# Attention and feed-forward block on one core: projections and transposes moved from full-height to 64-row TensorE tiles, attention outputs turned by VectorE

## The reference

```
h   = LN(x);  q, k, v = h @ w_q.T, h @ w_k.T, h @ w_v.T
a   = softmax(q k^T / 4) v   (per batch and head) ;  y = a @ w_o.T
x   = x + LN(y)
h   = LN(x);  prev = h shifted by one token (zeros for the first)
xr  = mu_r*h + (1-mu_r)*prev ;  xk = mu_k*h + (1-mu_k)*prev
r   = sigmoid(xr @ W_r.T) ;  kk = relu(xk @ W_k.T)^2
out = x + LN(r * (kk @ W_v.T))
```

## Time and profile before

| | |
|---|---|
| median of 3 runs | 1445.39 us |
| the profiled execution | 1448.0 us, its span 1446.2 us |
| PE, matmuls | 1354.5 us busy (94%), 8916 records |
| PE, weight loads | 607.8 us (42%) |
| ACT | 1015.3 us (70%) |
| DVE | 858.2 us (59%) |
| POOL | 299.2 us (21%) |
| granted TensorE clock, mean over the span | 0.983 |

### The profile page before, as it was taken

The page is one execution under the profiler, slowest core; times in us unless marked ns, Lnnn a source line. Parts: engine busy times, 40 slices in busy tenths (PEclk is TensorE's granted clock), DMA queues, the critical chain, the costliest instruction groups (busy, mean ns, idle before and its releaser), DMA issues.

```text
span 1446.2 us, 21872 instructions
## 1 busy us (share of the span) xinstructions
PE 1354.5 (94%) x8916; PEld 607.8 (42%) x8916; DVE 858.2 (59%) x1738; ACT 1015.3 (70%) x1080; POOL 299.2 (21%) x366
## 2 busy tenths in 40 slices
PE   3889999999999999999999999999999999999974
PEld 2433454444443444344443444444444444433433
DVE  5442575567647585565755666466754647463747
ACT  2558767777677677777777776776777777788751
POOL 7100211213111221212112222111311121211221
PEclk9999999999999999999999999999999999999996
DMA  3562534215232345115441152422442054301010
GB/s 131 143 161 86 113 64 103 59 60 116 63 86 59 108 82 106 43 44 132 88 103 49 56 130 45 103 59 75 101 94 61 23 131 88 75 2 30 1 30 15
DMA packets 61311, 112.79 MB, mean 78 GB/s; under 512 B 6400, under 2 KB 31232, under 8 KB 61184
## 3 DMA queue, kind: packets, MB, share of 16 engines
q1 hardware_dynamic: 61184, 111.05, 31.9%
HBM read 69.08 MB, written 41.94 MB: 77 GB/s over the span
## 4 chain that ended last, share of the span: by engine, by line
PE 79%; ACT 12%; DVE 7%; issue 1%; POOL 0%; DMA 0%
PE O L410 28%; PE M L193 25%; PE S L391 21%; ACT PT L398 11%; PE M L465 2%; PE M L442 2%; DVE A L561 1%; PE M L235 1%; DVE scratch L560 1%; DVE C L188 1%; DVE xA L227 1%; DVE scratch L576 0%; DVE B L188 0%; DVE p L264 0%; DVE Z L188 0%
## 5 line engine op out<-in xcount | busy, mean ns | idle before, releaser
L398 ACT ACTIVATE PT<-S 128x1024 f32<-128x1024 f32 x1024 | 983.9, 1024 | 318.1 <-PE S L391 318.1
L410 PE MATMUL O<-PT,V 128*17 128x512 f32 x4096 | 541.0, 600 | 0.0
L391 PE MATMUL S<-QS,KS 50*128 50x512 f32 x2048 | 417.3, 465 | 34.7 <-ACT PT L398 30.2
L391 PEld LDWEIGHTS S<-QS,KS 50*128 50x128 f32 x2048 | 169.8, 184 | 295.6 <-ACT PT L398 211.6
L193 PE MATMUL M<-WH,B 128*128 128x256 f32 x768 | 165.9, 298 | 14.0 <-DVE B L565 6.4
L193 PEld LDWEIGHTS M<-WH,B 128*128 128x128 f32 x768 | 127.6, 193 | 97.0 <-issue 39.5
L505 POOL TENSOR_SCALAR veh<-mvh 128x2 f32<-128x2 f32 x96 | 21.2, 221 | 583.3 <-DVE mvh L503 582.9
L410 PEld LDWEIGHTS O<-PT,V 128*17 128x17 f32 x4096 | 68.0, 95 | 160.1 <-issue 159.9
L193 PE MATMUL M<-WL,B 128*128 128x256 f32 x384 | 109.4, 285 | 0.0
L193 PE MATMUL M<-xnT,WH 128*128 128x512 f32 x256 | 92.8, 445 | 9.8 <-DVE xnT L243 9.8
L637 DVE RECIPROCAL Z<-Z 128x512 f32<-128x512 f32 x30 | 100.6, 3353 | 1.0
(11 more groups left out here) (101 smaller groups left out, 1263.6 us busy)
## 6 DMA issues: line engine op xcount, KB each, us to landing
scr<-p SPq DMA_DIRECT2D x124, 256.0 KB
QS<-scr SPq DMA_DIRECT2D x60, 256.0 KB, 5.0
KS<-scr SPq DMA_DIRECT2D x60, 256.0 KB, 7.0
QS<-scr SPq DMA_DIRECT2D x68, 128.0 KB, 4.3
KS<-scr SPq DMA_DIRECT2D x68, 128.0 KB, 7.3
xA<-x_dram SPq DMA_DIRECT2D x16, 512.0 KB, 7.1
xB<-x_dram SPq DMA_DIRECT2D x16, 512.0 KB, 7.6
out_dram<-xB SPq DMA_DIRECT2D x15, 512.0 KB, 3.5
```

Of the source, the lines that this page charges most:

```text
L391: fn = lambda e, p=p, a=a, rows=rows: e.matmul(PS[p][:, a, :], KS[qd][rows, p, kt * 128:kt * 128 + 128], QS[qd][rows, p, hf * 512:hf * 512 ...
L398: e_fn = lambda e, p=p: e.activation(PT[i % 2][:, 2 * p:2 * p + 2, :], PS[p][:, :, :], ACT.Exp, scale=SCALE)
L410: fn = lambda e, j=j: e.matmul(PO[g % 2][32 * j:32 * j + 17, :], V[b % 2][:, kt, 4 * qd + j, :], PT[i % 2][:, j, :], start=(kt == 0), stop ...
```

## The change

All projections and transposes are cut in two halves of 64 rows (a = 0 and a = 1), as the scores are. Half 0 of a block runs in rows 0 to 63 and half 1 in rows 64 to 127, both adding into the same bank; half 1 starts only after half 0 has finished, so that meanwhile half 0 of the next block runs beside it. There are three PM banks instead of two, and one PO bank instead of two. `pump`, called once a step between `scores(i+1)` and `values(i)`, gives each tile matmuls worth a quota of 0.68 (1.3 in the first 8 steps). A block enters when the operations that make its input have been issued. Orders by hand now list blocks alone; what follows a block is spread over the next steps at each REST.

The outputs of a quad are turned by DVE's transposes of 32x32 blocks out of PO (T), divided, and after each second quad turned once more and split into cT (the split's difference is POOL's); the order of w_o's rows is permuted to fit. The mixes are made in the order k, r with the first on A and C; the reciprocal of 512 columns is cut in two. The k activations go to C instead of Bf. o_x, o_xr, o_xk, o_act, o_sig and o_out go into what follows y, z, k, r and v. Spreads are issued at steps 12, 18, 26 instead of 16, 24, 27 (the first batch's at 9 instead of 12).

```diff
-STEPS, RATE = 29.00, 0.750
+TERMS = ((0, 0), (0, 1), (1, 0))
...
-        PO = [ctx.enter_context(nc.psum_tensor(f"O{i}", [128, 512], F32)) for i in range(2)]
-        PM = [ctx.enter_context(nc.psum_tensor(f"M{i}", [128, 512], F32)) for i in range(2)]
+        PO = ctx.enter_context(nc.psum_tensor("O", [128, 512], F32))
+        PM = [ctx.enter_context(nc.psum_tensor(f"M{i}", [128, 512], F32)) for i in range(3)]
...
+        def put(a):
+
+            cost, fn, waits = tile[a].pop(0)
+            spent[a] += cost
+            if tile[a]:
+                pe.quiet(fn, *waits)
+            else:
+                now[a].token = pe.op(fn, *waits)
+            if a == 0:
+                for block in halfway:
+                    block.behind += cost
+            if not tile[a]:
+                block, now[a] = now[a], None
+                if a == 0:
+                    halfway.append(block)
+                else:
+                    until_rest(block.done(block.bank, PM[block.bank], block.token))
+
+        def begin(a, wait):
+
+            if a == 0:
+                if not waiting or len(halfway) > 1 or (halfway and now[1] is not None):
+                    return False
+                ready, free = waiting[0].ready(), bank_free[made[0] % 3]
+                if ready is None or free is None:
+                    return False
+                block = waiting.popleft()
+                block.bank = made[0] % 3
+                bank_free[block.bank] = None
+                made[0] += 1
+                tile[0] = [(cost, fn, ()) for cost, fn in block.half(PM[block.bank], 0)]
+                tile[0][0] = (*tile[0][0][:2], (*ready, *free))
+            else:
+
+
+                if not halfway or not (halfway[0].behind > .3 or wait):
+                    return False
+                block = halfway.popleft()
+                tile[1] = [(cost, fn, ()) for cost, fn in block.half(PM[block.bank], 1)]
+                tile[1][0] = (*tile[1][0][:2], (block.token,))
+            now[a] = block
+            return True
+
+        def pump(quota):
+
+            due[0] += quota
+            for a in range(2):
+                spent[a] = max(spent[a], due[0] - 2 * quota)
+            while True:
+                stuck = 0
+                for a in sorted(range(2), key=lambda a: spent[a]):
+                    if not tile[a] and not begin(a, not tile[0]):
+                        stuck += 1
+                    elif spent[a] + tile[a][0][0] / 2 > due[0]:
+                        stuck += 1
+                    else:
+                        put(a)
+                        break
+                if stuck == 2:
+                    return
+
...
+        def feature_half(name, mt, moving):
+
+            n = W_NAMES.index(name)
+
+            def half(m, a):
+                rows, out = rows_of(a), []
+                for k, (c, (i, j)) in enumerate(itertools.product(range(2), TERMS)):
+                    w = (WH, WL)[i][rows, n, c, mt * 128:mt * 128 + 128]
+                    out.append((.216, lambda e, k=k, w=w, v=moving(j, c, rows): e.matmul(
+                        m[:, :], w, v, start=(a == 0 and k == 0), stop=(a == 1 and k == 5))))
+                return out
+            return half
+
+        def token_half(name, still):
+
+            n = W_NAMES.index(name)
+
+            def half(m, a):
+                rows, out = rows_of(a), []
+                for k, (t, c, (i, j)) in enumerate(itertools.product(range(2), range(2), TERMS)):
+                    w = (WH, WL)[j][rows, n, c, :]
+                    out.append((.117, lambda e, k=k, t=t, w=w, v=still(i, c, t, rows): e.matmul(
+                        m[:, t * 256:t * 256 + 256], v, w, start=(a == 0 and k == 0),
+                        stop=(a == 1 and k % 6 == 5), skip_group_check=True)))
+                return out
+            return half
+
+        def turn_half(src):
+
+            def half(m, a):
+                rows = rows_of(a)
+                return [(.109, lambda e, t=t: e.transpose(m[:, t * 128 + 64 * a:t * 128 + 64 * a + 64],
+                                                          src(t, rows), ident[rows, rows])) for t in range(4)]
+            return half
 
...
-                d = dve.op(lambda e: e.tensor_copy(On[g % 2][:, :], PO[g % 2][:, :]), pv_of[i], on_read.get(g - 2),
-                           split_of["wr"])
-                acc_free[g % 2] = d
-                on_ready[g] = d
-
+                until_rest(quad(g, qd))
+
+
+
+        def quad(g, qd):
+            at, half = T[g % 2], qd % 2
+            view = at[:, :].rearrange("p (y r) -> p y r", r=32)
+            d = dve.op(lambda e: e.transpose(at[:, :], PO[:, :]), pv_of[8 * g + 7], tk.get(("T", g % 2)),
+                       split_of["wr"])
+            tk["acc_free"] = d
+            if qd < 3:
+                yield REST
+            d = dve.op(lambda e: e.reciprocal(rec[:, :], view[:, :, 16]), d, tk.get("rec_read"))
+            over = rec[:, :].unsqueeze(2).to_broadcast([128, 16, 16])
+            d = dve.op(lambda e: e.tensor_tensor(CC[:, qd // 2, :, 16 * half:16 * half + 16], view[:, :, 0:16], over,
+                                                 ALU.mult), d, tk.get("CC_read"), *part_read[2])
+            tk["rec_read"] = tk["T", g % 2] = d
+            if not half:
+                return
+            yield REST
+            cols = slice(512 * (qd // 2), 512 * (qd // 2) + 512)
+            d = dve.op(lambda e: e.transpose(at[:, :], CC[:, qd // 2, :, :].rearrange("p y r -> p (y r)")), d)
+            tk["CC_read"] = d
+            d = copy(cT[0][:, cols], at[:, :], d, tk.get("cT_read"))
+            d = side().op(lambda e: e.tensor_tensor(cT[1][:, cols], at[:, :], cT[0][:, cols].bitcast(F32),
+                                                    ALU.subtract), d)
+            tk["T", g % 2] = tk["cT", g // 4, qd // 2] = d
 
...
+                d = copy(C[0][:, cols], A[:, cols], k, tk.get("C_read"))
+                tk["xk", u, c] = side().op(lambda e: e.tensor_tensor(
+                    C[1][:, cols], A[:, cols], C[0][:, cols].bitcast(F32), ALU.subtract), d)
+                lent_to.append((k1, diff, k))
...
+        FIRST = "V2 V3 Q10 K10 Q11 K11"
+        EVEN = "T00 T10 y0 y1 T01 T11 Q00 K00 z0 z1 Q01 K01 k0 k1 r0 r1 V0 v0 v1"
+        ODD = "Q10 K10 y0 y1 Q11 K11 z0 z1 V1 V2 k0 k1 r0 r1 V3 v0 v1"
+        QUOTA, FIRST_QUOTA = .68, 1.3
-        SPREAD_AT = (16, 24, 27)
+        SPREAD_AT = (12, 18, 26)
...
             for s in range(32):
                 i = 32 * u + s
                 if i + 1 < len(steps):
                     scores(i + 1)
-                values(i)
                 if s == 0 and u > 0:
                     load_xb(u - 1)
-                if s in NEW:
-                    o_turn(u, NEW.index(s))()
-                    spent += COST["ot"]
-                if cost == REST:
-                    cost = next(pieces, None)
-                while cost is not None and (cost <= 0 or spent + cost / 2 <= rate * (s + 1) or s == 31):
-                    if cost == REST and s < 31:
-                        break
-                    spent += max(cost, 0.0)
-                    cost = next(pieces, None)
+                pump(FIRST_QUOTA if u == 0 and s < 8 else QUOTA)
+                values(i)
+                again, resting[:] = resting[:], []
+                for work in again:
+                    until_rest(work)
                 if u == 0 and 3 <= s < 7:
                     split_weights([W_NAMES[s]])
-                if (u, s) == (0, 12):
+                if (u, s) == (0, 9):
                     spread(0, 2)
                     spread(0, 3)
...
```

More of the change, by code:

```diff
@@ new lines, in sandwich_kernel, with __init__, until_rest @@
+        tile = [[], []]
+        now = [None, None]
+        spent, due = [0.0, 0.0], [0.0]
+        made = [0]
+        resting = []
+        class Block:
+            def __init__(self, half, ready, done):
+                self.half, self.ready, self.done = half, ready, done
+                self.behind = 0.0
+        def until_rest(work):
+            for said in work or ():
+                if said == REST:
+                    resting.append(work)
+                    return
[15 more added lines that the diff above has]
+                    until_rest(block.done(block.bank, PM[block.bank], block.token))
@@ L499, in norm_stats, with have, ready @@
+        def have(*keys, more=(), queued=()):
+            def ready():
+                found = [tk.get(key) for key in keys]
+                return None if None in found or not all(key in tk for key in queued) else (*found, *(split_of[name] for name in more))
+            return ready
         def norm_stats(g, src, *ready):
@@ L551, in run, with mix, for_k @@
                 tk["z", c] = [d, d0]
-            return run
-        def o_xr(u, c):
-            def run():
+                if c:
+                    yield from mix(u)
```

(44 more changed lines are left out.)

395 lines of the change are left out of this document (142 added, 253 removed).

## The result

The changed kernel takes 1740.96 us (median of 4 runs, 1731.23 to 1748.49), the kernel before beside it 1444.89 (4 runs): a ratio of 1.2045, 95% interval 1.1974 to 1.2116. The prediction said 1343, 1282 to 1414. Lines Lnnn are now lines of the changed kernel: S L494, exps L501, O L513, matmuls of feature blocks L268 (512 columns a half) and of token blocks L281 (256), transposes on PE L291, DVE's transposes L530 and L544.

A forecast was written before the change was run, and what follows sets the result against it. The prediction took PE, busy 94% of the span, as the bound. Steps 845+321+36+22+8+5 = 1237, head 52, tail 55 and 1.8 around gave 1346, as median of runs 1343 us, range 1282 to 1414.

The forecast's parts named there:

- (2): Projection matmuls on PE split into 64-row halves: a pair priced as one whole matmul, 321 us with transposes; at worst 321 more.
- (4): Even dealing of matmuls to the tiles by quota 0.68 per step: unevenness costs 36 us, upper bound 72.
- rival D: Halves on PE do not overlap when weights change each time: 1664 us if none do, chance 0.03.
- (7): Half 1 waits for its half 0, PE's queue behind it: 8 us together with operand waits, bounds 0 and 30.
- rival A: Waits for DVE, at the single O bank and at projections' banks and operands, take the gain: 1415 us, chance 0.13.
- (5): DVE's load stays near 850 us, transposes 0.69 each; the difference moved to POOL, 1.69 each, is hidden.
- (3): Scores and projections on PE share a tile form, so entering projections costs nothing: step 2.28 us, 1166 for 512 steps.
- Rival B: Nothing is saved on PE's mode changes, each step pays 0.20 for entering projections: 1445 us, no change, chance 0.04.
- Rival C: PE is bound by its number of instructions, 59 ns each: step 2.51 us, total 1461, chance 0.06.
- (6): One PSUM bank for O instead of two, PE waiting for DVE to turn it: 22 us, bounds 0 and 96.
- (8): Head and tail, where blocks must run a half alone at each end: +6.5 and +2, making 52 and 55 us.
- (1): Turns of O and of the concatenated heads leave PE: 384 transposes, 42 us less.

The follow-up runs named there:

- couple_late2: Changed kernel with two blocks at a time, their halves laid in pairs, blocks taken up two steps late, quota 0.70: 1436.57 us, 0.9923 of the kernel before.
- couple_bulk: couple_late2 with one line changed, so that of every couple first tile 0's halves are queued, then tile 1's: 1656.92 us.
- paired: Changed kernel with another dealing: a stuck empty tile saves up no time, and tile 0 may start a block while one is halfway: 1546.11 us.
- first: Changed kernel, but an empty tile 0 is given its next block before tile 1 is asked: 1641.07 us.
- whole: Changed kernel with projection and transpose blocks at full height (128 rows, no halves), the rest of the change kept: 1486.82 us.
- whole_late2: whole with blocks taken up two steps after their operands were queued and quota 0.72 instead of 0.68: 1451.44 us.
- the three couples shown above: couple_late2 and two variants of it: couples begun a step after their banks' copies, with other edits (1484.25 us); y groups behind the second transposes (1462.01 us).

## Why the prediction was wrong, point by point

**(2), the price of halves: this step failed**, together with **(4)**. It rested on what pairs of scores show and took for granted that the halves of M would lie beside each other as those do. The hardware part holds: pairs start together, and 3964 halves cost what 1981 whole ones did (`couple_late2`), with new weights each time. What I did not do is follow `pump` into the queue. (4) priced unevenness as 36 us, with 72 as its bound and "a lone half block" in it; the queue makes 498-321 = 177. I had written the whole loss, 321 us, into (2) as its worst end, but left it out of the range and gave it, as rival D, 0.03, by a mechanism (weights change) that isn't the one. The order is: `couple_bulk` costs 220 by nothing but order, and `paired` takes back 195, of which some 43 belong to (7).

**(7), the end of half 0: 8 us expected, bounds 0 and 30.** "The plan puts 0.3 of other matmuls between" is true only where `wait` is false, which holds for 24 of 288. In the steps 194 have 0.3 to 0.6 us more between their second scores and O than the queue's prices; they sum to 94 us. Removing most of it gave 100 (`first`).

**Operands, rival A's mechanism, were there too.** 29 steps have over 1 us more than their prices, 89 us, the low clock behind a stand included. Six of them, 4.8 to 4.9 each, stand at the beginning of a batch, where y waits for POOL's difference of cT (32.5 us in all, the longest wait 4.7). Part (5) called that difference "hidden by the blocks queued between the last quad and y". POOL takes 1.30 each, less than the 1.69 assumed, but the cover was missing where y came next. What late take-up brought, 35 us in `whole` and 46 in `paired`, is about what such steps lose: their excess falls from 83 to 49 in the one and from 114 to 65 in the other. The chain after at one such place:

```profile
465.25 1.27 POOL cT L547
...
466.57 0.37 PE M L281
```

No matmul starts between 462.93 and 466.57. The clock is the third value from the end (ahead of DMA share and GB/s) in these stretches before, around and behind it:

```profile
455.00:462.90 7.90, 7.53 (x64) 4.08 (x57) 4.40 (x15) 6.06 (x7) 3.15 (x5) 1.00 0.00 1
464.50:471.30 6.80, 4.73 (x21) 2.62 (x22) 3.35 (x5) 0.91 (x1) 1.66 (x2) 0.50 0.83 187
471.40:480.00 8.60, 8.48 (x68) 4.89 (x67) 1.97 (x6) 5.60 (x7) 2.22 (x3) 1.00 0.79 154
```

It falls to 0.50 (1.2 GHz) in the stand and stays there for 4.7 us of work behind it.

**Account of the steps after,** from the starts, with M by the model: S and O 845, M 498, the two kinds of wait with smaller ones 202, slower S 25 and O 20: 1590, against 1588.9. Predicted: 845+321+36+22+8+5 = 1237. PE's clock is in these terms: 0.96 over the steps against 1.00, some 138 us at 1.2 GHz. No term of the sum had it.

**(3) holds in what it says of the entry.** S to M costs none (0.95 for 16 halves in `couple_late2`), while at full height it stands in most steps: 382 of `whole`'s have 0.1 to 0.3 us over their prices, 73 us in all. Rival B falls. But the whole gain isn't had: against `whole_late2` the couples have 30 us less in the steps (1353.0 against 1322.7) and 14 more in head and tail. A step of 2.28 left "a margin of 0.2" to ACT; that was too little, since S stands up to 54 us for exps in `couple_late2` by the account of starts.

**Rival C falls.** Sixteen halves with sixteen loads in 0.95 us are 30 ns an instruction, half of its 59. (Its 9.25 M matmuls a step count those of head and tail in; the steps have 4424, 8.6 each.)

**(5) holds in its durations, (6) in its range.** DVE and POOL after, the two transposes and the difference (busy us, mean ns):

```profile
L530 DVE STREAM_TRANSPOSE T<-O 128x512 f32<-128x512 f32 x64 | 45.2, 706 | 106.4 <-PE O L513 105.9
...
L544 DVE STREAM_TRANSPOSE T<-CC 128x512 f32<-128x512 f32 x32 | 22.7, 710 | 0.9
...
L547 POOL TENSOR_TENSOR cT<-T,cT 128x512 fp32r<-128x512 f32 x32 | 41.5, 1298 | 260.8 <-DVE cT L314 260.8
```

0.71 against 0.69 taken. The estimate of 1.24 that the prediction worked out from the Trainium skill's 311 ns (VectorE: DVE Perf Modes, The three transpose paths) is far above it, and the measurement decides. The single O bank was priced at 22 (0 to 96); it costs 12.8 to 38.1 in the waits of the three couples shown above, and nothing to speak of in the changed kernel, where PE is itself late.

**(8), head and tail: 52 and 55 expected, 60.6 and 79.9 measured.** The tail priced one lone half for V, 2.3, on top of the 4.64 of its 24 whole matmuls, and 1.4 for y. The chain after has, for V alone:

```profile
1711.58 2.94 PE M L281 x12
1714.57 4.82 PE M L281 x24
1719.42 2.94 PE M L281 x12
```

That is 10.7 for 48 halves, 0.20 to 0.25 each: the middle 24, which should have been twelve pairs, are issued twelve and twelve, so even here hardly any pair is formed, and y is laid in the same way. It is the failure of (2) once more, and not only the price of a lone half; the clock in the tail is 0.54 besides, before 0.73. `couple_late2` has 49.6 and 61.7.

**(1)** wasn't tried by itself.

So most of the loss comes from one assumption about the program, not about the chip: halves as dealt cost 254 of the 296 us. With pairs laid in order and blocks taken up two steps late the change is worth 0.8%, not the 7% predicted: the plain sum for couples is 845+310 = 1155, and the 168 above it are S held by exps (54), operands and banks (98) and slower O (18), with 61 us of low clock among them.

## What to carry to other kernels

Two row tiles share the array only if their matmuls are close in PE's queue, here at most four places apart; deal them as pairs, never by two separate budgets, and count the pairs in the queue or the trace before pricing the split. A dealer with arrears turns each stall into a bulk, and a lag with an exception is no lag: print the order it makes. As steps get shorter, look at what was hidden by the slack (a sigmoid's exps, a single bank, one difference on POOL) and move it first.

## What was unexpected of the hardware

Order alone, with the same instructions, moved the time from 1436.6 to 1656.9 us. Still, an idle row tile was served ahead of up to three matmuls of the busy one, never of more. A half 1 that waits for the end of its half 0 starts 0.45 us after the last matmul of it (512 columns), where one that follows alone starts after 0.23 and one in a pair at once; meanwhile no matmul of either tile starts. A stand of PE costs more than itself, by the low clock behind it: 0.96 over the steps of the changed kernel, 0.98 over those of `couple_late2`, before 1.00. A 32x32 transpose of 128x512 on DVE takes 0.706 us out of PSUM and 0.710 out of SBUF, hardly more than a copy out of PSUM (0.683).
